# Feed-forward products in high and low parts, and one variance chain for two layer norms, in a four-block transformer kernel

## The reference

```
x = x + linear_attention(ln(x))      # q,k,v: 256x256; elu+1; per head kv = k'v; out / normalizer; Wo
x = x + ffn(ln(x))                   # below
x = x + batch_attention(ln(x))       # 16 tokens of each batch attend, 3 iterations; others get the bias ob
x = x + ffn(ln(x))
def ffn(x):
    shared = square(relu(x @ Ws1)) @ Ws2       # 256 -> 128 -> 256
    logits = x @ Wr; prob = trunc(softmax of the two largest)
    return shared + sum_e prob[e] * (square(relu(x @ W1[e])) @ W2[e])
```

## Time and profile before

| | us |
|---|---|
| median of 3 runs | 457.77 (457.25 to 458.14) |
| profiled execution | 457.29 |
| its span, first to last instruction | 455.5 |
| PE busy | 425.2 (93%), 2570 matmul records |
| DVE busy | 293.2 (64%) |
| POOL busy | 203.5 (45%) |
| ACT busy | 183.8 (40%) |
| mean granted PE clock | 0.993 of full |

### The profile page before, as it was taken

The page is one execution under the profiler, slowest core; times in us unless marked ns, Lnnn a source line. Parts: engine busy times, 40 slices in busy tenths (PEclk is TensorE's granted clock), DMA queues, the critical chain, the costliest instruction groups (busy, mean ns, idle before and its releaser), DMA issues.

```text
span 455.5 us, 7618 instructions
## 1 busy us (share of the span) xinstructions
PE 425.2 (93%) x2570; PEld 354.7 (78%) x2570; DVE 293.2 (64%) x651; ACT 183.8 (40%) x321; POOL 203.5 (45%) x334
## 2 busy tenths in 40 slices
PE   7799989999999999688979999999999999999971
PEld 4689979998898999676858876878777787787851
DVE  4565575455556543459637697878858777887843
ACT  2464545555455541224134532333243323424440
POOL 3344442433334350036144367566527527635562
PEclk9999999999999999999999999999999999999997
DMA  8512111111100003100110111011010111011102
GB/s 260 179 48 78 63 47 46 48 46 46 46 0 1 0 2 89 8 2 3 51 46 4 50 49 35 15 48 47 4 47 1 50 48 35 16 49 47 48 32 71
DMA packets 22776, 20.58 MB, mean 45 GB/s; under 512 B 3255, under 2 KB 22717, under 8 KB 22717
## 3 DMA queue, kind: packets, MB, share of 16 engines
q1 hardware_dynamic: 22156, 19.32, 13.5%
q10 hardware_dynamic: 560, 0.52, 0.4%
HBM read 11.32 MB, written 8.45 MB: 43 GB/s over the span
## 4 chain that ended last, share of the span: by engine, by line
PE 82%; DVE 7%; ACT 5%; issue 2%; POOL 2%; DMA 1%; POOLq 0%; ACTq 0%; DVEq 0%
PE PG L1236 11%; PE PB L1356 6%; PE PT L1395 6%; PE PA L1356 5%; PE PB L1377 5%; PE PA L1425 4%; PE PA L1431 3%; PE PA L1426 3%; PE PA L1226 3%; PE PA L1227 3%; PE PA L1228 3%; PE PB L1214 3%; PE PB L1212 3%; PE PB L1213 3%; PE PT L1435 3%; PE PA L1367 3%
## 5 line engine op out<-in xcount | busy, mean ns | idle before, releaser
L454 POOL TENSOR_TENSOR ln_a<-ln_bn 128x4 f32<-128x4 f32 x32 | 6.5, 205 | 132.0 <-DVE ln_bn L934 132.0
L1236 PE MATMUL PG<-scratch 128*128 128x256 f32 x256 | 58.0, 379 | 1.3 <-DVE scratch L821 1.3
L821 DVE SCALAR_TENSOR_TENSOR scratch<-scratch,PB 128x1024 f32<-128x1024 f32 x16 | 19.5, 1221 | 60.3 <-ACT scratch L570 60.3
L1236 PEld LDWEIGHTS PG<-scratch 128*128 128x128 f32 x256 | 47.4, 190 | 7.4 <-issue 1.5
L535 ACT ACTIVATE scratch<-x_all,ln_shift,ln_rstd 128x255 f32 (+1 forms) x60 | 31.1, 589 | 36.7 <-PE PG L1236 30.2
L934 DVE BATCH_NORM_STATS2 ln_bn<-x_all 128x6 f32<-128x256 f32 x128 | 44.9, 413 | 0.9
L416 POOL TENSOR_SCALAR ln_rstd<-ln_mv 128x4 f32<-128x4 f32 x16 | 3.7, 228 | 91.3 <-DVE ln_mv L743 88.4
L1212 PE MATMUL PB<-wk_hi,xt_hi 128*128 128x256 f32 x128 | 39.0, 305 | 0.4 <-DVE xt_lo L768 0.4
L429 POOL TENSOR_TENSOR x_all<-x_all,scratch 128x1024 f32 (+1 forms) x16 | 38.2, 2388 | 0.6 <-ACT scratch L535 0.5
L429 POOL TENSOR_TENSOR x_all<-x_all,ob_rows 128x1024 f32<-128x1024 f32 x16 | 37.8, 2360 | 0.0
L695 ACT ACTIVATE scratch<-PA,ln_rsq 128x256 f32<-128x256 f32 x32 | 13.4, 471 | 59.3 <-PE PA L1356 35.4
(11 more groups left out here) (239 smaller groups left out, 1039.0 us busy)
## 6 DMA issues: line engine op xcount, KB each, us to landing
out_dram<-x_all SPq DMA_DIRECT2D x16, 512.0 KB, 3.1
x_all<-n_L_attn_a_inputs_q_dram SPq DMA_DIRECT2D x15, 512.0 KB, 3.6
x_all<-n_L_attn_a_inputs_q_dram ACTq DMA_DIRECT2D x2, 128.0 KB, 2.8
x_all<-n_L_attn_a_inputs_q_dram SPq DMA_DIRECT2D x2, 128.0 KB, 2.6
scratch<-in_L_attn_a_Wk_dram SPq DMA_DIRECT2D x1, 256.0 KB, 4.6
scratch<-in_L_attn_a_Wq_dram ACTq DMA_DIRECT2D x1, 256.0 KB, 5.0
scratch<-in_L_attn_a_Wv_dram SPq DMA_DIRECT2D x1, 256.0 KB, 6.8
scratch<-in_L_attn_a_Wo_dram SPq DMA_DIRECT2D x1, 256.0 KB, 6.2
```

Source lines behind the costliest of these rows:

```text
L1236: last = mm(PG[:, c, 0:D], k_tok[:, t, c * P:(c + 1) * P], xn[g % 2][:, t, :], start=(g == 0 and t == 0), stop=(g == G - 1 and t == T - 1))
```

## The change

It does five things.

1. **The feed-forward products are split.** The up product, wc by h2s, both calls of `down`, each become three fp32r products. For that w1c, wc and ws2 are split once in step 0 (three copies on ACT, three subtractions on the DVE), and x2t, h2s and h3 in every step. ACT makes all high parts (x2t_hi in two instructions of 512 columns, h2s_hi, h3_hi). POOL makes x2t_lo (two subtractions) and h3_lo, the DVE makes h2s_lo.
2. **One `rsq` for both slots.** POOL waits for bn2 of r and bn3 of v and then runs one chain over both, 8 elements a partition instead of twice 4.
3. **POOL's order** in a step is now h3_lo of v, the joined chain, x2t_lo of r, then L429, the batch attention's slot 1, L517 and slot 2 as before.
4. **Semaphores.** rsq2 and rsq3 become rsq23; several semaphores of the batch attention that were used once are merged into c_once, c_made and c_taken. New ones serve the split operands.
5. **Memory.** h2s now shares the memory of h2; w1c and ob_t lie early in h3, wc and colsum_w2t in y3; scratch is shorter, the raw weights of the batch attention swap halves of b_weights with the folded ones, and pass 1 has its weights in pieces of their own that the new fp32r operands reuse in pass 2.

The core of the diff, without the merged semaphores and the addresses:

```diff
@@ POOL
-            def rsq(slot, j, bn, powed, done):
...
-                nc.gpsimd.tensor_tensor(ln_rsq[:, slot, :], a, minus_ones[:, :], ALU.pow).then_inc(done, 1)
+            def rsq(slots, j, done):
+
+                a, d, both, out_ = ln_a[:, slots, :], ln_d[:, slots, :], ln_bn[:, slots, :, :], ln_rsq[:, slots, :]
...
+                nc.gpsimd.tensor_tensor(out_, a, minus_ones[:, slots, :], ALU.pow).then_inc(done, 1)
+
+            def x2_low(r):
+                for c in range(C):
+                    pool.wait_ge(x2_hi, C * r + c + 1)
+                    nc.gpsimd.tensor_tensor(x2t_lo[:, c, :], x2t[:, c, :], x2t_hi[:, c, :].bitcast(F32), ALU.subtract).then_inc(x2_lo, 1)
+
+            def h3_low(v):
+                pool.wait_ge(h3_hi_done, v + 1)
+                ge(pool, f4_mm, v)
+                nc.gpsimd.tensor_tensor(h3_lo[:, :], h3, h3_hi[:, :].bitcast(F32), ALU.subtract).then_inc(h3_lo_done, 1)
...
+                if runs(v):
+                    h3_low(v)
                 if runs(r):
+                    pool.wait_ge(bn2, T * (r + 1))
                     ge(pool, r2_mm, r)
-                    rsq(0, r, bn2, pow2, rsq2)
                 if runs(v):
+                    pool.wait_ge(bn3, T * (v + 1))
                     ge(pool, out_dve, 2 * v)
                     ge(pool, f4_scaled, 2 * v)
-                    rsq(1, v, bn3, pow3, rsq3)
+                if runs(r) or runs(v):
+                    rsq(slice(0 if runs(r) else 1, 2 if runs(v) else 1), i - 1, rsq23)
                 if runs(r):
+                    x2_low(r)
                     pool.wait_ge(t2_mm, C * (r + 1))
                     add_row(nr, ob_rows, ob_added)
@@ ACT
                         nc.scalar.activation(x2t[:, c, :], PA[:, c, :], ACT.Copy).then_inc(t2_done, 1)
+                    for c in range(C):
+                        act.wait_ge(t2_done, C * r + c + 1)
+                        nc.scalar.activation(x2t_hi[:, c, :], x2t[:, c, :], ACT.Copy).then_inc(x2_hi, 1)
...
+                    act.wait_ge(f1_scaled, r + 1)
+                    ge(act, f2_mm, r)
+                    nc.scalar.activation(h2s_hi[:, :], h2s, ACT.Copy).then_inc(h2_hi, 1)
...
+                    act.wait_ge(f3_sq, r + 1)
+                    ge(act, f4_mm, r)
+                    nc.scalar.activation(h3_hi[:, :], h3, ACT.Copy).then_inc(h3_hi_done, 1)
@@ DVE
-                    ge(dve, f2_mm, r)
                     nc.vector.tensor_tensor(h2s, h2, PT[:, 1, :], ALU.mult).then_inc(f1_scaled, 1)
+                    dve.wait_ge(h2_hi, r + 1)
+                    nc.vector.tensor_tensor(h2s_lo[:, :], h2s, h2s_hi[:, :].bitcast(F32), ALU.subtract).then_inc(h2_lo, 1)
@@ PE
-            def down(pair, h, done):
+            def down(pair, hi, lo, done):
                 for t in range(T):
-                    last = mm(four(pair)[:, t, :], h[:, t * P:(t + 1) * P], ws2[:, :], start=True, stop=True)
+                    dst, tile = four(pair)[:, t, :], slice(t * P, (t + 1) * P)
+                    mm(dst, hi[:, tile], ws2_hi[:, :], start=True, stop=False)
+                    mm(dst, hi[:, tile], ws2_lo[:, :], start=False, stop=False)
+                    last = mm(dst, lo[:, tile], ws2_hi[:, :], start=False, stop=True)
...
-                    pe.wait_ge(f3_sq, v + 1)
+                    pe.wait_ge(h3_lo_done, v + 1)
                     pe.wait_ge(t2_done, min(C * (r + 1), C * NG))
-                    down(PA, h3, f4_mm)
+                    down(PA, h3_hi, h3_lo, f4_mm)
...
                     for c in range(C):
-                        pe.wait_ge(t2_done, C * r + c + 1)
-                        last = mm(PT[:, 0, :], w1c[:, c, :], x2t[:, c, :], start=(c == 0), stop=(c == C - 1))
+                        pe.wait_ge(x2_hi, C * r + c + 1)
+                        mm(PT[:, 0, :], w1c_hi[:, c, :], x2t_hi[:, c, :], start=(c == 0), stop=False)
+                        mm(PT[:, 0, :], w1c_lo[:, c, :], x2t_hi[:, c, :], start=False, stop=False)
+                    for c in range(C):
+                        pe.wait_ge(x2_lo, C * r + c + 1)
+                        last = mm(PT[:, 0, :], w1c_hi[:, c, :], x2t_lo[:, c, :], start=False, stop=(c == C - 1))
                     last.then_inc(f1_mm, 1)
...
-                    pe.wait_ge(f1_scaled, r + 1)
-                    mm(PT[:, 0, :], wc, h2s, start=False, stop=True, skip_group_check=True).then_inc(f3_mm, 1)
+                    pe.wait_ge(h2_hi, r + 1)
+                    mm(PT[:, 0, :], wc_hi[:, :], h2s_hi[:, :], start=False, stop=False, skip_group_check=True)
+                    mm(PT[:, 0, :], wc_lo[:, :], h2s_hi[:, :], start=False, stop=False, skip_group_check=True)
+                    pe.wait_ge(h2_lo, r + 1)
+                    mm(PT[:, 0, :], wc_hi[:, :], h2s_lo[:, :], start=False, stop=True, skip_group_check=True).then_inc(f3_mm, 1)
...
-                    down(PB, h2s, f2_mm)
+                    down(PB, h2s_hi, h2s_lo, f2_mm)
```

More of the change, by code:

```diff
@@ L105, in hybrid_kernel, with parts, take @@
         r_gap = sb("r_gap", [P, 4, T])
-        SCR = 9 * 1024 + 8
+        SCR = 4 * T * D
         scratch = sb("scratch", [P, SCR])
[L110 to L116, removed]
+        def parts(piece):
+            at = [0]
+            def take(n):
+                a = piece[:, at[0]:at[0] + n]
+                at[0] += n
+                assert at[0] <= piece.shape[1]
+                return a
+            return take
+        part = parts(scratch)
         xn = [part(T * D).rearrange("p (t d) -> p t d", t=T) for _ in range(2)]
@@ L152, in hybrid_kernel @@
             xt_hi, xt_lo = sb1("xt_hi", [P, C, GT]), sb1("xt_lo", [P, C, GT])
+            part = parts(sb1("wvo", [P, 9 * D], F32))
+            g_sb = part(C * D).rearrange("p (c n) -> p c n", c=C)
+            wv = part(C * D).rearrange("p (c n) -> p c n", c=C)
+            bo_rows = part(D)
+            wo_raw = part(C * D).rearrange("p (c n) -> p c n", c=C)
+            wv_last, bv_rows = part(D), part(D)
+        w1c_hi, w1c_lo = sb("w1c_hi", [P, C, F], F32R), sb("w1c_lo", [P, C, F], F32R)
+        wc_hi, wc_lo = sb("wc_hi", [P, F], F32R), sb("wc_lo", [P, F], F32R)
+        ws2_hi, ws2_lo = sb("ws2_hi", [P, D], F32R), sb("ws2_lo", [P, D], F32R)
+        x2t_hi, x2t_lo = sb("x2t_hi", [P, C, GT], F32R), sb("x2t_lo", [P, C, GT], F32R)
+        h2s_hi, h2s_lo = sb("h2s_hi", [P, GT], F32R), sb("h2s_lo", [P, GT], F32R)
+        h3_hi, h3_lo = sb("h3_hi", [P, GT], F32R), sb("h3_lo", [P, GT], F32R)
+        early = parts(h3)
+        w1c = early(C * F).rearrange("p (c f) -> p c f", c=C)
+        ob_t = early(C * P).rearrange("p (c n) -> p c n", c=C)
+        early = parts(y3.rearrange("p t d -> p (t d)"))
+        wc = early(F)
+        colsum_w2t = early(F + C * F)
+        colsum, w2t = colsum_w2t[:, 0:F], colsum_w2t[:, F:].rearrange("p (c f) -> p c f", c=C)
+        h2s = h2
         b_weights = sb("b_weights", [P, 2, 4, C * D])
@@ L1146, in chain @@
                 elif at == (16, 1):
-                    dve.wait_ge(c_ffn, 1)
-                    nc.vector.tensor_tensor(x_s_out, PG[0:SP, 0, 0:D], xs, ALU.add).then_inc(c_added, 1)
-                    dve.wait_ge(c_added, 1)
+                    dve.wait_ge(c_once, FFN)
+                    nc.vector.tensor_tensor(x_s_out, PG[0:SP, 0, 0:D], xs, ALU.add).then_inc(c_made, 1)
+                    dve.wait_ge(c_made, ADDED)
             for g in range(G):
@@ L1547, in chain @@
                     if it == 2:
-                        pe.wait_ge(c_dsum, 1)
-                        mm(PG[0:SP, 0, D:D + 1], ones_f[0:SP, 0:SP], dsum[0:SP, 0:1], start=True, stop=True).then_inc(c_diff, 1)
+                        pe.wait_ge(c_made, DSUM)
+                        mm(PG[0:SP, 0, D:D + 1], ones_f[0:SP, 0:SP], dsum[0:SP, 0:1], start=True, stop=True).then_inc(c_once, 1)
                 if at == (14, 1):
@@ L1565, in chain @@
                         last = mm(PG[:, 1, 0:SP], ws1[:, c, :], xs_t[:, c, :], start=(c == 0), stop=(c == C - 1))
-                    last.then_inc(c_hid, 1)
+                    last.then_inc(c_once, 1)
                 elif at == (16, 1):
-                    pe.wait_ge(c_sq, 1)
-                    mm(PG[0:SP, 0, 0:D], h_s, ws2[:, :], start=True, stop=True).then_inc(c_ffn, 1)
+                    pe.wait_ge(c_taken, 5)
+                    mm(PG[0:SP, 0, 0:D], h_s, ws2[:, :], start=True, stop=True).then_inc(c_once, 1)
             for g in range(G):
```

191 lines of the change are left out of this document (103 added, 88 removed).

## The result

The changed kernel takes 499.52 us (median of 4 runs, 499.18 to 499.89), the kernel before, beside it, 457.95 (457.25 to 459.12): a ratio of 1.0905 [1.088, 1.093]. The forecast was 486 (470 to 497): the direction and the loop were right, the size 13.5 us short.

The account below looks back on a forecast made before the run. It took a loop through four engines, closed by POOL's low half of x2t, as the bound: fifteen loops 242.1 plus batch attention 24.0 less 241.0, with start and tail 3.95, add 29 to 457.3: 486 us, range 470 to 497.

Parts of the forecast that it names:

- the loop: Pass 2, one up product's end to the next through PE, DVE, ACT and POOL: 16.14 us a step, against 16.06 before.
- plain loops: Steps of pass 2 for which the forecast adds no batch attention work: 16.14 us each.
- the extras of the batch attention: Batch attention work in slots 2 and 3 of DVE and PE that lengthens steps: 24.0 us in all, bounds 12 and 30.
- Rivals 1 to 3: PE stays the bound, 441 us (0.07); batch attention hides behind POOL, 474 (0.10); power of eight costs as four, 476 (0.08).
- rival 5: The PE idles some 3 us a step and its clock falls, by a tenth: 492 us, chance 0.05.
- the 4 us of PE links: The PE's share of each pass 2 loop; with a tenth of the clock gone it would lose 0.4 us a loop.
- the last F: F is the end of a step's up product (L1395) in pass 2; fifteen loops lie between first and last.
- Start and tail: Step 0 copies and later first up product, plus 0.85 us after the last one: 3.95 us in all, bounds 1 and 6.
- rival 4: POOL's power of sixteen locks out the DVE's h2s_lo in steps 7, 10, 12: 3.6 us in all, 490 us, chance 0.12.

Follow-up runs that it names:

- fill: Changed kernel with 141 zero-weight products on the PE ahead of its waits for the low halves, in 14 steps: 487.66 us, 1.0676 of the kernel before.
- join_only: Kernel before with one edit, the two variance chains joined into one that waits for both statistics: 463.6 us, ratio 1.0132.
- h3_only: Only the second `down` (into PA) split, two separate chains, other products float32, changed kernel's semaphores and most of its layout: 462.52 us, 1.0101 of the kernel before.
- x2lo_dve: Changed kernel with both x2t_lo subtractions moved from POOL to the DVE, first in its step, joined chain kept: 470.51 us, 1.029 of the kernel before.
- up_f32: Changed kernel with the up product back in float32, joined chain and the other split products kept: 463.52 us, 1.0129 of the kernel before.
- up_f32_two_fill2: Changed kernel with float32 up product, two separate chains and six unread products in the PE's step 2 wait: 458.76 us, 1.0039 of the kernel before.

## Why the prediction was right, and where it was wrong

**Right: what bounds, and the loop.** The third up product waits for POOL's `x2t_lo`, POOL's chain for the second statistics. With the clock at full in every loop (`fill`), the loops take 266.9 us against a forecast of 266.1. Two errors cancel in that: the plain loops of `fill` (16.33, 16.32, 16.50, 16.67, 16.32) average 16.43 where I had 16.14, which is 4.3 over fifteen, and the extras of the batch attention are then 20.4, not 24.0. That the sum of the loops came out so near is luck to that extent.

**Right: single prices.** The power of eight elements came out at 1.649 us for 1.66, the low half at 1.287 for 1.276:

```profile
L493 POOL TENSOR_TENSOR x2t_lo<-scratch,x2t_hi 128x512 fp32r<-128x512 f32 x32 | 40.5, 1287 | 0.0
...
L488 POOL TENSOR_TENSOR ln_rsq<-ln_a,minus_ones 128x8 f32<-128x8 f32 x15 | 24.7, 1649 | 1.2
```

Twelve products of a `down` go by in 1.43 us, counted between weight loads (L1425 at 351.11 to L1438 at 352.54), as forecast. Rivals 1 to 3 fall with these: the PE is no bound, the extras did not hide, and the power does not cost as four.

**Wrong: rival 5, the clock.** This is the step that failed. I had "the 4 us of PE links would lose 0.4 a loop", 6 us in all, at a chance of 0.05; it was 12.2 in the loops and 1.4 behind the last one between the profiled executions, 10.5 to 12 by all runs, shown by `fill`. That is most of the 13.5 us by which the forecast was short, or all of it. Two things were wrong in it. I argued from one stretch, 225 to 236.6 us, that 3 us of idle PE leave the clock alone. Those 3 us are two waits, of 1.80 and 1.17 us, in one step; the changed kernel has a wait of 1.7 to 2.5 us in ten of its loops, and the clock fell at nine of them. And I spread the loss as a tenth over the PE's links. In the trace it comes as stretches at half speed, which begin at or close behind the third up product, so that L1479 and L1484, on which `o_hi` and everything behind it wait, run in them. I should have priced it by such stretches: some 39 us at the lower level ahead of the last F cost 12.2 us, 0.3 us for each. The price is uneven: the first ten loops lost only 2.4 us against `fill` for 15 us at the lower level, the last five 9.8 for 24. Why the later ones cost more is not shown.

**Wrong, small: what I put at nothing.** The joined chain I booked as worth nothing by itself, and h3_lo as hidden by POOL's idle time. With the PE still the bound the one costs 6 us (`join_only`), and the other makes the kernel some 5 us slower although it comes with a shorter `down` (`h3_only`). About 2.5 us of each are step 2 to 3, by way of L969 on the DVE and the clock after it; the rest lies in other steps, and its cause is not shown. I had looked at POOL's idle time and at the second `down`, not at who wants the early chain. In the changed kernel the loop through POOL is longer than either, and the loops of `fill` came out at the forecast, so I count no part of the 13.5 us here.

**Start and tail.** The first F came 2.6 us late for 3.1. The tail lost 0.5 without the clock (`fill`: 16.3 for 15.84) for 0.85.

**The lock (rival 4) is wrong for the power, right for its neighbour.** Both were in the trace, the power at 294.7 us (and at 310.8 and 364.0), the subtraction at 405.9:

```profile
294.69 2.91 POOL L525 TENSOR_TENSOR b_weights<-b_weights,minus_half 64x16 f32<-64x16 f32 x1
...
295.30 0.69 DVE L1050 TENSOR_TENSOR h2s_lo<-scratch,h2s_hi 128x512 fp32r<-128x512 f32 x1 [0.70 <-ACT h2s_hi L760]
...
405.93 1.29 POOL L557 TENSOR_TENSOR x_all<-x_all,scratch 128x512 f32<-128x512 f32 x1
405.94 1.84 DVE L1050 TENSOR_TENSOR h2s_lo<-scratch,h2s_hi 128x512 fp32r<-128x512 f32 x1 [0.70 <-ACT h2s_hi L760]
```

Under the power of sixteen, which lasts 2.91 us, `h2s_lo` with its two SBUF inputs takes its usual 0.69 all three times; beside the subtraction L557 it takes 1.84, and ends 0.56 after it. The Trainium skill (SBUF — State Buffer, Who interferes with whom) says that a DVE instruction with two SBUF inputs contends with a GpSimd instruction that reads SBUF, and calls the port that they share an exclusive lock. For L557 the trace agrees to 0.13 us (0.69 after its end would be 407.91, the end was at 407.78), for the power it disagrees. So rival 4's 3.6 us did not come.

**What stays open.** Of the 29 to 31 us that are not clock, the runs give the up product's low half on POOL the bulk (`x2lo_dve` takes it off POOL, with some 13 us left to the kernel before), but shares of join, extras and `h2s_lo` can't be added up: `join_only` and `up_f32` both cost 6 although one contains the other. Nor do these runs show why one wait of 1.84 us left the clock alone and nine like it did not.

## What to carry to other kernels

An idle engine is not free capacity: ask when in the step its input comes and when its output is wanted, and add the links up to a loop, since a loop between engines can be the bound while no engine is busy all the time. Joining two chains saves their fixed cost and makes the early half as late as the late one, so it needs its own line in the sum. And when a change makes TensorE wait in most steps, price the granted clock by whole stretches at half speed behind each wait, above all in front of the work that feeds the other engines, and test it with a kernel that keeps TensorE multiplying through the wait.

## What the runs showed of the hardware

- The changed kernel's PE waits for the low half ten times for 1.7 to 2.5 us ahead of the last F. At nine of these the granted clock falls to 0.50, at one of 1.84 us it stays at 1.00, as it does at waits of 1.56, 1.80 and 1.17 us within one step of the kernel before. Products by a zero weight in the waits brought all loops to 1.00 and 10.5 to 12 us back.
- The same kernel can differ by its clock alone: `up_f32_two_fill2` took 458.1 to 458.5 us in six runs at 0.991 to 0.992, and 461.3 to 463.6 in three at 0.975 to 0.982.
- A power on GpSimd grows with the elements per partition: 1.015 us at four, 1.649 at eight, 2.905 at sixteen (the four of L525, on 64 partitions); a multiplication of eight in its place takes 0.20.
- GpSimd's power left a DVE subtraction with two SBUF inputs alone in three cases of three (0.69 us each); GpSimd's subtraction of 128x512, in the one case here, held it for nearly its whole length (1.84).
